# Packed words for PE and ScalarE: one word for 16 counting steps and one for four destination scores, unpacked in registers, in a four-layer graph network

## The chip, the cores and the metric

One NeuronCore of a Trainium2 chip runs the whole program. The metric is the device time of one execution in microseconds. The kernel is written instruction by instruction, with semaphores between the engines: PE (TensorE), DVE (VectorE), ACT (ScalarE), POOL (GpSimd) and SP (SyncE, which only issues DMAs).

## The reference, cut to what matters

There are 1875 nodes with 256 features and 60,000 edges (src, dst) sorted by dst. Each of four layers computes a graph operation and then x = layernorm(x + layer(x)). The change lies in the first layer and in the counting that serves the later ones:

```
feat = einsum('ni,rhid->rnhd', x, W)                 # 8 relations, 4 heads of 64
el = sum(feat[type, src] * attn_l[type], -1)         # score of the source
er = sum(feat[type, dst] * attn_r[type], -1)         # score of the destination
e = leaky_relu(el + er); alpha = softmax of e over the edges with the same dst
h = segment_sum(alpha * feat[type, src], dst)        # GAT layer
segment_sum(msg[src], dst)                           # layers 2 and 3: relation sums, mean
```

In layers 2 and 3 the kernel multiplies by a dense count matrix: for each destination, how many edges come from each source (two relations). This matrix is what the counting walk makes.

## The kernel before

**Windows and steps.** Destinations are taken in WINS = 118 windows of 16. The sorted edges are cut into STEPS = 586 steps of up to 128 edges; a step lies in one window, and the window of a step never falls and rises by at most one from step to step. The array WS (one number a step, the same on all partitions) holds the window of each step. The engines learn it by loading numbers from on-chip memory into their registers: `offsets(engine, step, n, most, table)` loads n numbers of a table with one instruction (line 361 of the profile).

**Order of the stages.** (1) Up to 53 us: loading and the tables of steps. (2) 53 to 154 us: the feature table (8 relations by 1875 rows) on PE, written to device memory. (3) 166 to 398 us: the destination scores. (4) 398 to 421 us: transposes and a few matmuls. (5) 421 to 994 us: the counting walk. (6) 994 to 1315 us: softmax and the weighted sums of the first layer. (7) To the end: the other layers with the count matrix, all dense.

**Destination scores.** PG = 4 columns of edges are a group, of which there are NG = 32. For each group PE broadcasts the keys of the edges into PSUM (`broadcast_keys(g)`, L1548 and L1550), DVE and ACT turn them into one-hots (L1038, L1042 on DVE; L602, L604 copy on ACT), and PE multiplies them with a piece of the table ERW of 12 columns (`er_group(g)`, L1562): SC = 5 matmuls for each of the four columns, or four from group 19 on; 19 x 20 + 13 x 16 = 588. Which piece is the window's: an offset of 12 columns times the window. The 20 offsets of a group are loaded as 32-bit numbers from the table OFFP, which DVE fills early (L935, L938). DVE sums the results (L1047).

**Counting walk.** For each step DVE makes two one-hots (L1068 with 128 columns, L1069 with 480) in a ring of AS = 8 and signals `a_oh`; PE multiplies them into the PSUM bank of the window (L1600). A ring of CBANKS = 4 banks serves the windows: before a step PE waits for `a_free` to be at least the window's number plus one, and takes bank (window + 1) mod 4. ACT reads the bank of a finished window (L630), clears the bank (L589) and signals `a_free`. ACT knows how many steps a window has from the table ENDS, of one number a window, eight to a load (L627). PE's table CT holds 512 times (window + 1) as 16-bit numbers, eight to a load. 8 steps stand ahead of a loop of 18 turns with AU = 32 steps each, and 2 behind it.

**Gathers.** Beside stages 3 to 5 POOL gathers rows of the feature table for the edges with indirect DMAs (L546, 469 in all) into a ring of NPL = 6 places. ACT copies the scores out of each place (`collect`, L585), which gives the place back to POOL and to SP, which writes the rows on (L417). ACT does its collects at fixed places of its own order: behind its copies of each group in stage 3, behind certain windows in the walk (`due`).

## Time and profile before

| what | value |
|---|---|
| timed runs, median | 2030.09 us (2027.18 to 2038.34, n = 3) |
| profiled execution, its own time | 2011.49 us |
| its span | 2009.8 us |
| mean granted clock of PE | 0.765 |
| busy: PE, DVE, ACT, POOL | 69%, 49%, 27%, 24% |
| chain that ended last: PE, DVE, issue | 54%, 18%, 17% |

Busy is what an engine's instructions took of the span; register instructions and loads into registers are not counted in it. "Issue" is time in which an engine waited for nothing that the profile shows. The chain is followed back from the last instruction to what released each. The rows ahead of the prediction are from the profiled execution.

### The profile page before, as it was taken

How to read it: one execution, taken by the hardware profiler on the slowest of the kernel's cores; microseconds unless marked ns; L12 is line 12 of the kernel's file. 1: busy time of each engine (PE TensorE's matmuls, PEld its weight loads, DVE VectorE, ACT ScalarE, POOL GpSimd, SP SyncE). 2: the span in 40 equal slices, each digit the busy share in tenths (PEclk: the TensorE clock that was granted, in tenths of full speed). 3: DMA queues.
4: the chain of work that ended last, by engine and by line, in shares of the span. 5: the costliest groups of instructions: out<-in, count | busy, mean ns of one | idle time of the engine just before them, and what ended most of it. 6: DMA issues, size and time to landing. Idle time of an engine off the chain costs nothing.

```text
span 2009.8 us, 21459 instructions
## 1 busy us (share of the span) xinstructions
PE 1387.4 (69%) x5399; PEld 735.2 (37%) x5400; DVE 978.3 (49%) x2436; ACT 552.5 (27%) x856; POOL 486.8 (24%) x517
## 2 busy tenths in 40 slices
PE   5894676576654444333418999978999989989930
PEld 3342343221111100000207777744444544554620
DVE  5413334246654444333398998864081460360636
ACT  1331222101222222222300000024775436427121
POOL 0005565531454566565300000000000000000022
PEclk9996555576665655555657999988999989989975
DMA  3534555531344555555406888600000010000022
GB/s 145 169 142 159 178 164 161 176 96 53 119 143 139 159 168 173 176 166 161 139 22 225 281 269 275 205 1 23 1 1 1 0 32 1 1 11 1 2 60 60
DMA packets 84507, 223.92 MB, mean 111 GB/s; under 512 B 18456, under 2 KB 27588, under 8 KB 83908
## 3 DMA queue, kind: packets, MB, share of 16 engines
q1 hardware_dynamic: 60452, 158.01, 22.7%
q0 software_dynamic: 23968, 64.77, 12.2%
q8 instruction: 53, 0.87, 0.2%
q14 instruction: 34, 0.28, 0.0%
HBM read 140.09 MB, written 82.63 MB: 111 GB/s over the span
## 4 chain that ended last, share of the span: by engine, by line
PE 54%; DVE 18%; issue 17%; another core or an unknown queue 5%; ACT 3%; DMA 2%; POOL 0%; SPq 0%; ACTq 0%; DVEq 0%; POOLq 0%
PE bank L1729 15%; PE bank L1666 11%; PE bank L1600 7%; PE bank L1519 5%; DVE arena L1069 5%; PE bank L1749 2%; DVE arena L1098 2%; PE bank L1548 2%; PE bank L1562 2%; PE bank L1713 2%; DVE arena L1068 1%; PE bank L1688 1%; PE bank L1818 1%; DMA arena<-in_xT 1%
## 5 line engine op out<-in xcount | busy, mean ns | idle before, releaser
L546 POOL DMA_INDIRECT arena<-feat_table,arena x469 | 450.1, 960 | 482.9 <-ACT arena L585 251.3
L1600 PE MATMUL bank<-arena 128*128 128x480 f16 x586 | 261.4, 550 | 309.9 <-issue 275.9
L1068 DVE TENSOR_SCALAR arena<-iota,arena 128x128 f16<-128x128 f16 x586 | 155.1, 265 | 302.8 <-PE bank L1600 205.6
L1729 PE MATMUL bank<-arena 128*128 128x472 f16 x1440 | 292.5, 367 | 9.3 <-DVE arena L1248 5.4
L1600 PEld LDWEIGHTS bank<-arena 128*128 128x128 f16 x586 | 60.3, 103 | 511.4 <-issue 510.9
L554 POOL DMA_INDIRECT arena<-al_table,edge_ends x15 | 14.4, 962 | 952.7 <-DMA al_table<-arena 948.4
L1666 PE MATMUL bank<-arena 128*128 x966 | 229.5, 392 | 0.7 <-issue 0.3
L1069 DVE TENSOR_SCALAR arena<-iota,arena 128x480 f16<-128x480 f16 x586 | 204.0, 348 | 0.0
L1729 PEld LDWEIGHTS bank<-arena 128*128 128x128 bf16 x1440 | 141.9, 99 | 159.7 <-issue 12.8
L1666 PEld LDWEIGHTS bank<-arena 128*128 128x128 f32 x966 | 174.5, 190 | 55.9 <-issue 34.6
L630 ACT ACTIVATE adjacency<-bank 128x480 uint16<-128x480 f32 x118 | 67.3, 570 | 442.3 <-PE bank L1600 382.6
L1154 DVE TENSOR_TENSOR arena<-arena 128x1024 f32<-128x1024 f32 x118 | 140.4, 1214 | 14.3 <-DMA arena<-edge_rows 12.6
L717 ACT ACTIVATE arena<-adjacency 128x1888 f16<-128x1888 uint16 x30 | 108.8, 3630 | 45.0 <-PE bank L1729 45.0
L698 ACT ACTIVATE arena<-adjacency 128x1888 f16<-128x1888 uint16 x30 | 109.0, 3637 | 34.6 <-PE bank L1729 34.6
L1519 PE MATMUL bank<-arena 128*128 128x512 f32 x240 | 111.3, 619 | 5.8 <-ACT arena L577 3.0
L1562 PE MATMUL bank<-arena 128*128 x588 | 76.8, 188 | 51.8 <-issue 46.2
L1548 PE MATMUL bank<-adjacency,ident 128*128 128x512 f16 x128 | 67.1, 617 | 42.1 <-DVE arena L1038 36.5
L1562 PEld LDWEIGHTS bank<-arena 128*128 128x128 f16 x588 | 59.3, 105 | 84.8 <-issue 72.7
L602 ACT ACTIVATE arena<-bank 128x512 f16<-128x512 f32 x64 | 35.7, 595 | 187.8 <-remote 122.2
L1161 DVE TENSOR_TENSOR arena<-iota,arena 128x1024 f32<-128x1024 f16 (+1 forms) x61 | 73.8, 1210 | 8.3 <-PE bank L1666 8.2
L1269 DVE COPY arena<-bank 128x472 f32<-128x472 f32 x12 | 7.0, 642 | 143.3 <-PE bank L1729 143.3
L1047 DVE TENSOR_REDUCE arena<-bank 128x80 f32<-128x240 f32 x32 | 13.0, 405 | 125.5 <-remote 85.8
(289 smaller groups left out, 1496.6 us busy)
## 6 DMA issues: line engine op xcount, KB each, us to landing
arena<-edge_rows SPq DMA_DIRECT2D x117, 520.0 KB, 4.7
edge_rows<-arena SPq DMA_DIRECT2D x67, 520.0 KB
edge_rows<-arena SPq DMA_DIRECT2D x67, 390.0 KB
feat_table<-arena SPq DMA_DIRECT2D x60, 260.0 KB, 2.1
arena<-feat_table,arena POOLq DMA_INDIRECT x469
arena<-in_w SPq DMA_DIRECT2D x1, 2048.0 KB, 9.7
arena<-in_xT SPq DMA_DIRECT2D x1, 1920.0 KB, 18.2
arena<-in_x SPq DMA_DIRECT2D x1, 1792.0 KB
```

What stands on the lines that cost most here:

```text
L546: g.indirect_dma_start(out=PLACE[k][:, t - lo, :], out_offset=None, in_=feat_t, in_offset=bass.IndirectOffsetOnAxis(ap=IE[:, t:t + 1], axi ...
L698: a.activation(chunk(CH1, c % 2, wide), ADJ[:, r, :].rearrange("p (n s) -> p n s", s=SH)[:, :, sh], ACT.Copy).then_inc(s["chunk_ready"], 1)
L717: a.activation(chunk(CH2, c % 2, wide), ADJ[:, 0, :].rearrange("p (n s) -> p n s", s=SH)[:, :, c], ACT.Copy).then_inc(s["chunk_ready"], 1)
L1068: v.tensor_scalar(OHS[st % AS], iota128[:, :], lo, None, ALU.is_equal)
L1069: v.tensor_scalar(OHK[st % AS], iota480[:, :], key, None, ALU.is_equal).then_inc(s["a_oh"], 1)
L1154: v.tensor_tensor(rows, rows, al, ALU.mult).then_inc(s["r_wgt"], 1)
L1519: ins = mm(PS[c][:, :], XT0[:, k, P * t:P * (t + 1)], W0[:, k, 512 * c:512 * (c + 1)], start=(k == 0), stop=(k == 1))
L1548: ins = mm(PS[j][:, 0:SFULL * P], row, KEY16[:, 0:SFULL, :].rearrange("p c e -> p (c e)"), start=True, stop=True)
L1562: ins = mm(PS[4 + g % 2][:, 3 * H * k:3 * H * (k + 1)], KO[g % 3][:, lo:lo + P], ERW[:, bass.ds(offs[k], 3 * H)], start=True, stop=True)
L1600: mm(CBANK[:, bass.ds(at, R2 * KW)], OHS[st % AS], OHK[st % AS], start=False, stop=False, skip_group_check=True)\
L1666: mm(BANKS[:, bass.ds(out_at, D)], OHR[:, (st // RG) % ORING, P * (st % RG):P * (st % RG + 1)], FBf[:, bass.ds(places[st % RK] >> 12, D)], ...
L1729: ins = mm(PS[4 * fo + j][:, 0:CW], m[:, P * fo:P * (fo + 1)], ch[:, CW * j:CW * (j + 1)], start=(c == 0 and q == 0), stop=(c == n - 1 and ...
```

## The change

**PE, counting.** CT becomes a 32-bit table with one word for CWORD = 16 steps, 38 words. Its low 7 bits are the window (plus one) of the first of these steps, and each of the 15 bits above says whether the window rises at the next step. PE adds the bits up in a register, step by step. A turn loads two words with one instruction. To make words and turns fit, the table begins 8 steps ahead of the first step. The bank's address is now worked out from the window: shift by 9, mask.

**PE, destination scores.** OFFP holds one word for the same matmul of the four columns of a group, four windows of 7 bits; five words a group are loaded, and PE shifts, masks and multiplies by 12.

**ACT.** ENDS holds two numbers of 12 bits in a word; a load takes four words for eight windows.

**DVE** makes the packed tables. OFFP and CT are now made ahead of the wait for `er_ld`, some 30 small operations; before, OFFP was made earlier (L935, L938) and CT after the scores (L1064).

```diff
-assert CBANKS >= 3 and AS % CLOAD == 0 and AU % CLOAD == 0 and 512 * WINS < 2 ** 16 and STEPS % 2 == 0 and CBANKS & (CBANKS - 1) == 0
+WBITS = 7
+WFULL = 2 ** WBITS
+CWORD = 16
+CROWS = -(-(STEPS + AS) // CWORD)
+EBITS = 12
...
-        CT = ar(A_WI, STEPS // 2).bitcast(U16)
+        CT = ar(A_WI, CROWS).bitcast(I32)
...
                 if w % CLOAD == 0:
-                    ends = nc.values_load_multi_w_load_instructions(
-                        ENDS[0:1, w:w + min(CLOAD, WINS - w)], engines=[ACTE], min_val=1, max_val=STEPS)[1]
-                act.wait_ge(s["a_mm"], ends[w % CLOAD])
+                    ends = offsets(ACTE, w // 2, min(CLOAD, WINS - w) // 2, STEPS * (2 ** EBITS + 1), ENDS)
+                act.wait_ge(s["a_mm"], ends[w % CLOAD // 2] >> (EBITS * (w % 2)) & (2 ** EBITS - 1))
...
-            v.tensor_copy(ENDS[0:1, 0:WINS], PS[4][0:1, 1:WINS + 1]).then_inc(s["ends_ready"], 1)
+            BEG = TMP[0:1, 1024:1024 + WINS]
+            link(v.tensor_copy(BEG, PS[4][0:1, 1:WINS + 1]))
+            BEGv = BEG.rearrange("p (w k) -> p w k", k=2)
+            v.scalar_tensor_tensor(ENDS, BEGv[:, :, 1], float(2 ** EBITS), BEGv[:, :, 0], ALU.mult, ALU.add).then_inc(s["ends_ready"], 1)
...
-            link(v.memset(OFFP, 0))
-            for c in range(SC):
-                n = min(P, STEPS - P * c)
-                v.tensor_scalar(OFFP.rearrange("p (a c) -> p a c", c=SC)[:, 0:n, c], WS[:, P * c:P * c + n], float(3 * H), None, ALU.mult)
...
+            OFFF = OFFW.rearrange("p c g j -> p (c g j)")
+            link(v.memset(OFFF, 0))
+            link(v.tensor_copy(OFFF[:, 0:STEPS], WS))
+            OPv = OFFP.rearrange("p (g c) -> p c g", c=SC)
+            OTv = OFFT.rearrange("p (g c) -> p c g", c=SC)
+            link(v.tensor_copy(OPv, OFFW[:, :, :, 0]))
+            for j in range(1, PG):
+                link(v.tensor_single_scalar(OTv, OFFW[:, :, :, j], WBITS * j, ALU.logical_shift_left))
+                link(v.tensor_tensor(OFFP, OFFP, OFFT, ALU.bitwise_or))
+            CWP = TMP[:, 640:640 + CWORD * CROWS]
+            CDF = TMP[:, 1280:1280 + CWORD * CROWS]
+            POW = TMP[:, 1920:1920 + CWORD]
+            link(v.memset(CWP, 0.0))
+            v.tensor_copy(CWP[:, CWORD - AS:CWORD - AS + STEPS], WS)
+            v.tensor_scalar(CWP[:, CWORD - AS + STEPS:CWORD * CROWS], CWP[:, CWORD - AS + STEPS:CWORD * CROWS], float(WINS - 1), None, ALU.add)
+            for u in range(CWORD):
+                ins = v.memset(POW[:, u:u + 1], float(WFULL * 2 ** (u - 1)) if u else 0.0)
+            link(ins)
+            v.memset(CDF[:, 0:1], 0.0)
+            link(v.tensor_tensor(CDF[:, 1:CWORD * CROWS], CWP[:, 1:CWORD * CROWS], CWP[:, 0:CWORD * CROWS - 1], ALU.subtract))
+            CDv = CDF.rearrange("p (b u) -> p b u", u=CWORD)
+            link(v.tensor_tensor(CDv, CDv, POW.rearrange("p (a u) -> p a u", a=1).to_broadcast([P, CROWS, CWORD]), ALU.mult))
+            link(v.tensor_reduce(CDF[:, 0:CROWS], CDv, AX.X, ALU.add))
+            v.scalar_tensor_tensor(CT, CWP.rearrange("p (b u) -> p b u", u=CWORD)[:, :, 0], 1.0, CDF[:, 0:CROWS], ALU.add, ALU.add)\
+             .then_inc(s["counts_table"], 1)
             dve.wait_ge(s["er_ld"], 16)
...
-            v.tensor_scalar(CT, WS, 1.0, 512.0, ALU.add, ALU.mult).then_inc(s["counts_table"], 1)
...
-                offs = offsets(PE, PG * SC * g, PG * SC, 3 * H * (WINS - 1), OFFP)
+                words = offsets(PE, SC * g, SC, WFULL ** PG - 1, OFFP)
...
+                        off = nc.s_assert_within((words[c] >> (WBITS * j) & (WFULL - 1)) * (3 * H), 0, 3 * H * (WINS - 1),
+                                                 skip_runtime_bounds_check_because="a window's number times the width of its scores")
                         ins = mm(PS[4 + g % 2][:, 3 * H * k:3 * H * (k + 1)], KO[g % 3][:, lo:lo + P],
-                                 ERW[:, bass.ds(offs[k], 3 * H)], start=True, stop=True)
+                                 ERW[:, bass.ds(off, 3 * H)], start=True, stop=True)
...
-            most = 512 * WINS
-
-            def count(i, st, word):
+            def count(i, st, window):
 
                 pe.wait_ge(s["a_oh"], i * AU + (st + 1))
-                pe.wait_ge(s["a_free"], word >> 9)
-                at = nc.s_assert_within(word & (512 * (CBANKS - 1)), 0, 512 * (CBANKS - 1), skip_runtime_bounds_check_because="a bank of the window's ring")
+                pe.wait_ge(s["a_free"], window)
+                at = nc.s_assert_within((window << 9) & (512 * (CBANKS - 1)), 0, 512 * (CBANKS - 1),
+                                        skip_runtime_bounds_check_because="a bank of the windows' ring")
                 mm(CBANK[:, bass.ds(at, R2 * KW)], OHS[st % AS], OHK[st % AS], start=False, stop=False, skip_group_check=True)\
                     .then_inc(s["a_mm"], 1)
 
-            words = offsets(PE, 0, AS, most, CT)
-            for st in range(AS):
-                count(0, st, words[st])
+            def count_word(i, word, st0, lo, hi):
+
+                window = word & (WFULL - 1)
+                for u in range(hi):
+                    if u:
+                        window = window + (word >> (WBITS + u - 1) & 1)
+                    if u >= lo:
+                        count(i, st0 + u, window)
+
+            most = 2 ** (WBITS + CWORD - 1) - 1
+            count_word(0, offsets(PE, 0, 1, most, CT)[0], -AS, AS, CWORD)
             with pe.Fori(0, A_N) as i:
-                for u in range(AU):
-                    if u % CLOAD == 0:
-                        words = offsets(PE, i * AU + (AS + u), CLOAD, most, CT)
-                    count(i, AS + u, words[u % CLOAD])
-            words = offsets(PE, AS + A_N * AU, STEPS - AS - A_N * AU, most, CT)
-            for st in range(AS + A_N * AU, STEPS):
-                count(0, st, words[st - AS - A_N * AU])
+                for k, word in enumerate(offsets(PE, i * 2 + 1, 2, most, CT)):
+                    count_word(i, word, AS + CWORD * k, 0, CWORD)
+            count_word(0, offsets(PE, 2 * A_N + 1, 1, most, CT)[0], AS + A_N * AU, 0, STEPS - AS - A_N * AU)
```

## Rows read from the trace of the kernel before

**Rows 1.** Busy time by stretch: us, then PE, PEld, DVE, ACT, POOL; PEclk, DMA, GB/s
```profile
166.00:398.00 232.00, 139.17 (x784) 79.86 (x782) 73.20 (x129) 48.00 (x121) 140.48 (x148) 0.51 0.55 171
421.00:575.00 154.00, 93.94 (x222) 22.77 (x220) 97.08 (x437) 22.63 (x56) 49.39 (x52) 0.64 0.28 88
575.00:994.00 419.00, 169.13 (x369) 38.13 (x369) 169.39 (x739) 108.13 (x264) 238.79 (x250) 0.56 0.51 160
```

**Rows 2.** Timeline of PE, early counting walk: start, duration, then the instructions
```profile
423.05 1.58 PE L1600 MATMUL bank<-arena 128*128 128x480 f16 x7
...
439.81 3.54 PE L1600 MATMUL bank<-arena 128*128 128x480 f16 x8 [1.96 <-issue]
445.26 3.54 PE L1600 MATMUL bank<-arena 128*128 128x480 f16 x8 [1.92 <-issue]
451.15 3.57 PE L1600 MATMUL bank<-arena 128*128 128x480 f16 x8 [2.35 <-issue]
```

**Rows 3.** PE's sequencer by source line: ns min/median/max of one, first and last start
```profile
L361 PEldq TENSOR_LOAD <-arena x74: 155/1922/2911, 419.5 to 992.8; - x74
...
L361 PEldq TENSOR_LOAD <-adjacency x32: 1356/1362/2438, 166.6 to 392.3; - x32
...
L361 PEldq TENSOR_LOAD <-arena x121: 330/333/779, 1071.8 to 1305.1; - x121
...
L1598 PEldq ALU_OP  x586: 2/36/1394, 421.8 to 993.7; - x196
...
L1600 PEldq ALU_OP  x586: 2/36/1395, 421.9 to 993.8; - x196
L1600 PEldq FUSED_REGOPS  x586: 1/46/1396, 422.0 to 993.9; - x196
...
L1562 PEldq FUSED_REGOPS  x588: 2/46/1397, 168.0 to 395.8; - x196
...
L1666 PEldq FUSED_REGOPS  x966: 42/60/103, 1073.1 to 1306.9; - x194
...
L1666 PEldq ALU_OP  x483: 32/32/32, 1073.3 to 1306.8; - x161
```

**Rows 4.** Groups: L1600 in 575 to 994, L630 over the span; busy, idle before
```profile
L1600 PE MATMUL bank<-arena 128*128 128x480 f16 x369 | 169.2, 559 | 250.1 <-issue 225.0 <-ACT bank L589 19.5 <-DVE arena L1069 4.6
...
L630 ACT ACTIVATE adjacency<-bank 128x480 uint16<-128x480 f32 x118 | 67.3, 570 | 442.3 <-PE bank L1600 382.6
```

**Rows 5.** Timelines of PE and of POOL in the late walk
```profile
765.65 0.56 PE L1600 MATMUL bank<-arena 128*128 128x480 f16 x1 [2.23 <-issue]
770.58 0.56 PE L1600 MATMUL bank<-arena 128*128 128x480 f16 x1 [4.37 <-issue]
...
751.00 0.94 POOL L546 DMA_INDIRECT arena<-feat_table,arena  x1 [1.68 <-issue]
...
771.41 0.94 POOL L546 DMA_INDIRECT arena<-feat_table,arena  x1 [0.30 <-issue]
```

**Rows 6.** Timeline of PE in the destination scores
```profile
207.00 2.76 PE L1562 MATMUL bank<-arena 128*128 x20 [0.91 <-DVE arena L1047]
...
211.79 2.31 PE L1562 MATMUL bank<-arena 128*128 x20
...
299.03 0.17 PE L1562 MATMUL bank<-arena 128*128 x1 [1.22 <-issue]
```

**Rows 7.** DVE before its first comparison, and the nearest prices (by source line)
```profile
164.28 1.42 DVE L1038 TENSOR_SCALAR arena<-bank,pcol 128x512 f16<-128x512 f32 x2 [0.83 <-PE bank L1550]
...
L935 DVE MEMSET adjacency<- x1: 592/592/592, 73.3 to 73.3; 128x640 int32 x1
...
L957 DVE TENSOR_TENSOR arena<-adjacency x1: 770/770/770, 87.4 to 87.4; 128x586 f32<-128x586 f32 x1
...
L1003 DVE TENSOR_TENSOR scores<-scores,iota x1: 261/261/261, 155.9 to 155.9; 1x110 int32<-1x110 int32 x1
```

**Rows 8.** DMA queues in the walk, 450 to 990: packets, MB, share
```profile
q14 instruction: 8, 0.07, 0.0%
```

More of the change, by code:

```diff
@@ L269, in build @@
         HB = ar(A_HB, D)
[L270 removed]
+        ENDS = ar(A_HB, WINS // 2)[0:1, :].bitcast(I32)
         OHR = ar(A_OR, ORING, RG * P)
@@ L274, in build @@
         KEY16 = EARLY[:, 47 * Q:47 * Q + SC * P // 2].bitcast(F16).rearrange("p (c e) -> p c e", e=P)
-        OFFP = EARLY[:, 45 * Q + 8:45 * Q + 8 + P * SC].bitcast(I32)
+        OFFW = TMP[:, 0:P * SC].bitcast(I32).rearrange("p (c g j) -> p c g j", c=SC, j=PG)
+        OFFP, OFFT = (EARLY[:, 45 * Q + 8 + NG * SC * k:45 * Q + 8 + NG * SC * (k + 1)].bitcast(I32) for k in range(2))
         ERF = EARLY[:, 48 * Q:48 * Q + WINS * H].rearrange("p (w h) -> p w h", h=H)
```

2 lines of the change are left out of this document (1 added, 1 removed).

## The prediction

> **What bounds the kernel now.** I read the windows by stage first. The change touches three stretches: the destination scores (166 to 398 us), the first part of the counting walk (421 to 575) and its rest (575 to 994) [rows 1]. In none of them is an engine full. PE is busy 139 of 232 us, 94 of 154 and 169 of 419, DVE less or about as much, and POOL, with its gathers, 140, 49 and 239. So the order of work inside a stretch decides, and the timeline shows it.
>
> In the early walk PE runs eight steps in 3.54 us and then stands 1.92 us before the next eight; where a turn of 32 ends, 2.35 us [rows 2]. Two things are to be seen. The eight steps are (3.54 - 0.58) / 7 = 0.42 us apart, although seven matmuls of the same form that had been queued up ran in 1.58 us, 0.2 us apart: the spacing in the loop comes from what PE's sequencer does between matmuls. And the pause of 1.92 us has the length of the median load of eight 16-bit words [rows 3]. A turn of 32 steps takes 3 x 5.45 + 5.89 = 22.2 us, 0.69 us a step; 154 us for 218 steps is 0.71. DVE's pair of one-hots and ScalarE's clearing follow PE there.
>
> The rest of the walk takes 419 / 368 = 1.14 us a step. PE idles 250 us before its matmuls, 225 of them "issue" [rows 4]: the engine waits for its own instruction stream. The timeline shows a second speed: at 765.65 and 770.58 single steps stand 4.9 us apart, within a run of 17 gathers on POOL, unbroken from 751.00 to 772.35, 20.41 / 16 = 1.28 us each [rows 5]. In the same way matmuls of the destination scores, usually 0.11 us apart, come at 1.4 us [rows 6]. Slow stretches occur only late in such long runs of gathers; early in the walk, with short runs, there are none. What is in them costs about 0.7 us for each instruction of PE's stream, whatever it does: 1.40 us for a matmul with one register instruction.
>
> **Price of a register instruction.** A destination-score matmul is preceded by one register instruction, a counting step by four (a sum for a_oh in line 1597, a shift in 1598, mask and address in 1600) [rows 3]. (2.31 - 0.19) / 19 = 0.11 us against 0.42, so each is (0.42 - 0.11) / 3 = 0.10 us. The 36 and 46 ns of the rows are the busy part only; three times 36 would give a step of 0.22 us, which is not seen.
>
> **Counting, early part.** After the change a step with u > 0 needs: the sum for a_oh, the shift, the mask with 1, the addition to the window, the shift by 9, the mask of the ring, the address: 7. The first step of a word needs 5. If the compiler folds pairs (in line 1666 one ALU and two fused instructions do the two addresses, shift and mask of two matmuls [rows 3]) it may be 5. I take 7, since the semaphore waits stand between the groups and a mask followed by an addition has no pair of that kind here. Turn after: 30 x 0.72 + 2 x 0.52 = 22.6, and in place of four loads at 1.92 one of two words; four 32-bit words take 0.33 [rows 3], and the branch 0.44 (2.35 - 1.92), so 23.4 us against 22.2. Over 218 steps, 6.8 turns, that is +8 us. Bounds: 5 instructions a step give 32 x 0.52 + 0.8 = 17.4 us, -32 us; 8 give +30.
>
> A page of the Trainium skill ("DMA: Bandwidth & Descriptors", the table of latencies and other measured facts) puts the floor of a tensor_load at about 600 ns. The trace has 0.33 us for four words, so it doesn't agree and the measurement decides. By the page each turn would be 0.27 us longer, an estimated +5 us over the 18 turns.
>
> **Counting, late part.** If x steps run at 4.2 us (six instructions by 0.7) and the others at 0.69, 4.2x + 0.69(368 - x) = 419 gives x = 47, or some 195 us of slow stretches. A slow step after has nine instructions, 6.3 us. If the slow time stays 195 us, 31 steps fall into it and 337 x 0.73 = 246 us follow: 441, +22. But POOL needs 250 x 1.28 = 320 us whatever PE does, PE in fast mode comes closer to its pace (0.73 us a step against 0.87 of gathers), and the runs of gathers, which start when ScalarE collects behind PE, may get shorter. I take +15, between 0 and +110 (all 47 steps stay slow: 47 x 2.1 = 99, and 11).
>
> **Destination scores.** A group of 20 matmuls takes 4.79 us now (207.00 to 211.79) [rows 6], one of 16 about 0.45 less; 19 and 13 of them are 147 us, and the stretch has 232: 85 us are slow. Added are a mask for the lowest number of a word, shift and mask for the three others: 1.75 x 0.10 = 0.175 us a matmul, 3.5 or 2.8 us a group (bounds 0, if all folds, and 3 instructions, 6 us). The load falls from 20 words, 1.36 us [rows 3], to five at about 0.35; half of it lies beside the broadcasts' matmuls, so -0.5. Fast groups then take 7.8 and 6.6 us, 234 us in all, as much as the stretch does now with its slow parts. POOL's part is 148 x 1.28 = 189 us; at 4.6 gathers, 5.9 us, a group it would no longer outrun PE, and its runs break up. With no slow time left the stretch stands still (+2). With half of it, 42 us at 2.6 us a matmul does only 16 of 588, +38. With all of it +75. I take +25, nearer to none, because the short runs of the early walk had none.
>
> **DVE's chain for the tables.** Some 30 small operations are put ahead of the wait for er_ld, and DVE waits only 0.83 us for PE before its first comparison at 164.28 [rows 7]. By their nearest rows: two memsets and two copies of some 600 numbers at no more than 0.59; a strided copy and six operations on 160 integers at 0.26; three passes over 608 at 0.77; the last 0.2: 6.7 us. For 16 memsets of one column the nearest row is the 0.26 of 110 integers, so 0 to 4 us; being one column each I take 0.05, 0.8. 7.5 less the 0.83: +6 (between 4 and 10). All that follows starts by so much later; PE's and ScalarE's first group wait for these comparisons. The operations taken out lay ahead of a wait of DVE for PE or beside PE's work: nothing.
>
> **ScalarE.** Its loads of eight words become loads of four, and each window has one or two register instructions more. It waits for PE 382 us in the walk [rows 4], so both are hidden while PE is the late one. In slow stretches its instructions too can cost 0.7, on one window in three of those steps; a few us, inside the bounds.
>
> **Sum.** 6 + 25 + 8 + 15 = +54 us. The profiled execution took 2011 us, the median of the timed runs is 2030, 0.9% more; 2011 + 54 = 2065 becomes 2084 against the median. I write 2085.
>
> **Rivals.**
> (a) The loads win: the compiler folds shift, mask and addition so that a step needs 5 and a matmul of the scores one or two. For it speaks line 1666. Early -32, late about -40 (368 / 218 of the early gain, less what the gathers hold), scores -5, DVE +6: -70, 1960; at 6 instructions a step about -20, 2010. It decides once a step has at most 6. Against it: word >> 9 and the ring's mask are two ALU instructions now, not folded.
> (b) The gathers set the pace: POOL's 1.28 us each bound both late stretches, and PE's added time falls into what were slow stretches. +6 +0 +8 -5, about +9: 2030 to 2040, no change to be told.
> (c) The slow stretches hold the same steps, each with more instructions at 0.7 us: +6 + 75 + 8 + 60 to 110, 2180 to 2230; half-way 2150. The price per instruction speaks for it; against it, that the runs of gathers end by POOL's own ring.
> (d) The turn's code grows from some 200 to some 290 instructions. In the walk there is practically no instruction traffic now, 8 packets [rows 8]: the turn stays resident. If it didn't, 18 turns would fetch; a pause like the longest load's, 2.9 us at most [rows 3], makes +50 us at the outside, on top of mine, 2135. "Runtime: NRT & Kernel Launch" of the Trainium skill, under Instruction fetch mechanics, says a taken branch to a page outside the window waits for a fetch; by the trace the rule has no case so far.
>
> **How the numbers follow.** My own case 0.54, with a range of 2043 (scores +2, late 0) to 2130; (a) 0.17; (b) 0.13; (c) 0.12; (d) 0.04. About 10 us, 0.5%, is what a measurement tells from no change. Faster 0.17, all of (a). Same 0.14: (b), and the edge of mine. Slower 0.69. The range of 8 in 10 leaves out the better half of (a) and the upper half of (c): 2005 to 2155.
>
> **What would show it.** Bursts of eight with pauses of 1.92 us are gone, and matmuls of line 1600's successor stand 0.72 us apart over 16 steps (0.5 would be rival a, and 0.42 free registers). The early walk takes about 162 us. Score matmuls stand 0.28 us apart in fast groups; the stretch from DVE's first comparison to the transposes is 235 to 270 us. DVE's first comparison starts near 170. Late single steps in long runs of gathers are 6 us apart; their total time tells (b), mine and (c) apart. Instruction-queue packets in the walk tell (d). I am wrong if a step has six register instructions or fewer, or if the slow stretches, which I know only by where they occur, answer to something else than the count of instructions.

## The result and the profile after

The changed kernel takes 2143.5 us (median; 2135.3 to 2151.2, n = 4) against 2029.8 us: ratio 1.056, 95% interval 1.051 to 1.060. It is 114 us slower. The forecast was +55 us (2085), so the side was right and the time stands within the range, but the loss is twice what was forecast. The profiled execution took 2135.3 us with a span of 2133.6, against 2011.5 and 2009.8: 124 us. That is 10 more than between the medians, because the profiled execution of the kernel before lies 18 us under its own median and that of the changed one 8 under; which stretch holds the 10 us can't be told.

From the page of the changed kernel: PE's clock in 40 slices, the chain that ended last by engine, and the gathers and the walk's matmuls (busy, mean ns, idle before and its releaser).

```profile
PEclk9995555565555555555555799999899989999975
...
PE 62%; issue 21%; DVE 13%; DMA 2%; ACT 1%; POOL 0%; SPq 0%; another core or an unknown queue 0%; DVEq 0%; ACTq 0%; POOLq 0%
...
L552 POOL DMA_INDIRECT arena<-feat_table,arena x469 | 449.1, 958 | 601.5 <-ACT arena L591 365.1
L1629 PE MATMUL bank<-arena 128*128 128x480 f16 x586 | 335.1, 576 | 289.6 <-issue 233.4
```

The same two groups of the kernel before:

```profile
L546 POOL DMA_INDIRECT arena<-feat_table,arena x469 | 450.1, 960 | 482.9 <-ACT arena L585 251.3
L1600 PE MATMUL bank<-arena 128*128 128x480 f16 x586 | 261.4, 550 | 309.9 <-issue 275.9
```

"Issue" has gone from 17 to 21% of the chain, PE from 54 to 62%. The matmuls of the walk are busy 335 us in place of 261, although they are the same matmuls. A little of it is the clock: more of them run at the lower one (mean 576 ns in place of 550, 586 x 26 ns = 15 us). The rest is how busy time is counted: at 0.42 us apart matmuls of 0.58 us overlap and the overlap counts once, at 0.73 us apart they don't overlap. POOL idles 119 us more, 114 of it until ScalarE's collects: the gathers are not what was late.

Windows that end with the first and the last matmul of each stretch tell where the 124 us are. First the changed kernel (scores, first 218 steps, the other 368; us, busy and count of these matmuls, granted clock, DMA share, GB/s), then the same stretches of the kernel before.

```profile
171.17:460.62 289.45, 102.64 (x588) 0.50 0.42 132
...
489.87:661.61 171.74, 123.25 (x218) 0.51 0.25 80
661.61:1114.64 453.03, 211.86 (x368) 0.50 0.47 146
```

```profile
168.12:396.08 227.96, 76.77 (x588) 0.50 0.54 169
...
423.04:579.01 155.97, 92.88 (x218) 0.63 0.28 90
579.01:994.64 415.63, 168.55 (x368) 0.56 0.51 159
```

Scores +61.5 us, first 218 steps +15.8, the others +37.4, together 114.7. The first score matmul starts 3.1 us later (168.12 to 171.17), between scores and walk there are 2.3 us more (29.25 against 26.96), and behind the walk 3.8 more. That makes 123.8.

DVE's first comparison, against [rows 7]:

```profile
167.16 1.41 DVE L1067 TENSOR_SCALAR arena<-bank,pcol 128x512 f16<-128x512 f32 x2 [0.83 <-PE bank L1578]
```

It starts 2.9 us later, with the same wait of 0.83 us.

The timeline of PE in fast groups of the scores (two groups of 16), and in the walk:

```profile
449.15 1.51 PE L1592 MATMUL bank<-arena 128*128 x6
450.83 1.17 PE L1592 MATMUL bank<-arena 128*128 x4 [0.17 <-issue]
...
455.58 1.59 PE L1592 MATMUL bank<-arena 128*128 x6 [1.43 <-DVE arena L1076]
...
499.73 1.29 PE L1629 MATMUL bank<-arena 128*128 128x480 f16 x2 [0.16 <-issue]
501.18 1.29 PE L1629 MATMUL bank<-arena 128*128 128x480 f16 x2 [0.17 <-issue]
```

Inside a word a score matmul now comes every (1.17 - 0.19) / 3 = 0.33 us (0.11 before), and a group of 16 every 6.4 us (449.15 to 455.58), a counting step every 1.45 / 2 = 0.73 us. The gaps say "issue".

The sequencer's rows, against [rows 3]: the scores' (L1592), then the sum for a_oh, the window's three instructions and its wait, and bank and address.

```profile
L1592 PEldq ALU_OP  x1029: 2/36/1388, 170.9 to 460.2; - x172
L1592 PEldq FUSED_REGOPS  x588: 2/55/709, 171.1 to 460.3; - x196
...
L1625 PEldq ALU_OP  x558: 1/36/1410, 493.2 to 1111.7; - x186
...
L1626 PEldq ALU_OP  x1692: 1/36/724, 483.3 to 1113.6; - x188
...
L1629 PEldq ALU_OP  x1172: 1/36/730, 485.1 to 1113.8; - x196
L1629 PEldq FUSED_REGOPS  x586: 1/46/723, 485.3 to 1113.9; - x196
```

1029 + 588 instructions for 588 matmuls are 2.75 each; 558 + 1692 + 1172 + 586 for 586 steps are 6.8 each. The compiler folded nothing of what I had left open.

The loads (two words at an odd place for the walk, four on ScalarE, five for the scores):

```profile
L367 PEldq TENSOR_LOAD <-arena x18: 3/534/909, 492.0 to 1070.7; - x18
L367 ACTq TENSOR_LOAD <-arena x14: 305/308/709, 584.8 to 1096.3; - x14
...
L367 PEldq TENSOR_LOAD <-adjacency x32: 584/1234/2045, 169.4 to 454.0; - x32
```

The two-word load takes 0.53 us and not 0.33, the five-word load 1.23 and not 0.35: it is hardly shorter than the 20 words before. Not every five-word load is that dear. The words of group g begin at word 5 x g of the table, and in e1 below, which has the same loads, those of g = 0, 4, 8 and so on to 28, which begin at a multiple of four words, take 0.59 to 0.63 us, and the 24 others 1.23 or more. This is the one of g = 4:

```profile
L367 PEldq TENSOR_LOAD <-adjacency x1: 601/601/601, 211.6 to 211.6; - x1
```

The late walk has slow stretches as before; this is the timeline of PE in one:

```profile
764.72 1.29 PE L1629 MATMUL bank<-arena 128*128 128x480 f16 x2 [0.17 <-issue]
768.95 0.58 PE L1629 MATMUL bank<-arena 128*128 128x480 f16 x1 [2.94 <-issue]
771.83 0.58 PE L1629 MATMUL bank<-arena 128*128 128x480 f16 x1 [2.31 <-issue]
775.95 0.56 PE L1629 MATMUL bank<-arena 128*128 128x480 f16 x1 [3.54 <-issue]
```

Single steps are 2.9 to 4.2 us apart, less than the 4.9 of [rows 5], though each now has seven register instructions in place of four. Over the last 368 steps, those that start more than 1.2 us after the one before, with no load between, number 51 in the trace before (155 us in all) and 73 in this one (222 us): 3.0 us each in both.

### The profile page after: what moved, and what is told of

Its sections match the earlier page's. It is cut to its first block, busy times and chain, and to the rows that moved or that the text cites. A ratio compares the mean times of both kernels' runs of the same rounds, so it can differ in the third digit from the quotient of the medians.

```text
span 2133.6 us, 24047 instructions
## 1 busy us (share of the span) xinstructions
PE 1489.2 (70%) x5399; PEld 743.5 (35%) x5400; DVE 1027.0 (48%) x2463; ACT 551.9 (26%) x856; POOL 485.9 (23%) x517
## 4 chain that ended last, share of the span: by engine, by line
PE 62%; issue 21%; DVE 13%; DMA 2%; ACT 1%; POOL 0%; SPq 0%; another core or an unknown queue 0%; DVEq 0%; ACTq 0%; POOLq 0%
PE bank L1762 14%; PE bank L1629 13%; PE bank L1699 10%; PE bank L1547 5%; PE bank L1592 4%; PE bank L1576 3%; DVE arena L1097 3%; PE bank L1782 2%; DVE arena L1126 2%; PE bank L1746 1%; PE bank L1721 1%; PE bank L1619 1%; PE bank L1851 1%; PE bank L1848 1%; DMA arena<-in_xT 1%
## 5 line engine op out<-in xcount | busy, mean ns | idle before, releaser
L1629 PE MATMUL bank<-arena 128*128 128x480 f16 x586 | 335.1, 576 | 289.6 <-issue 233.4
L1699 PE MATMUL bank<-arena 128*128 x966 | 228.6, 393 | 1.0 <-issue 0.4
L1097 DVE TENSOR_SCALAR arena<-iota,arena 128x480 f16<-128x480 f16 x586 | 208.9, 357 | 0.0
L1699 PEld LDWEIGHTS bank<-arena 128*128 128x128 f32 x966 | 175.4, 191 | 54.5 <-issue 32.7
L1592 PE MATMUL bank<-arena 128*128 x588 | 102.6, 188 | 130.7 <-issue 85.9
L1592 PEld LDWEIGHTS bank<-arena 128*128 128x128 f16 x588 | 59.8, 107 | 187.7 <-issue 181.8
L608 ACT ACTIVATE arena<-bank 128x512 f16<-128x512 f32 x64 | 34.9, 595 | 253.0 <-PE bank L1578 134.2
L1076 DVE TENSOR_REDUCE arena<-bank 128x80 f32<-128x240 f32 x32 | 13.0, 408 | 171.7 <-PE bank L1592 163.8
```

The lines of the kernel that those rows point to most:

```text
L1097: v.tensor_scalar(OHK[st % AS], iota480[:, :], key, None, ALU.is_equal).then_inc(s["a_oh"], 1)
L1592: ins = mm(PS[4 + g % 2][:, 3 * H * k:3 * H * (k + 1)], KO[g % 3][:, lo:lo + P], ERW[:, bass.ds(off, 3 * H)], start=True, stop=True)
L1629: mm(CBANK[:, bass.ds(at, R2 * KW)], OHS[st % AS], OHK[st % AS], start=False, stop=False, skip_group_check=True)\
L1699: mm(BANKS[:, bass.ds(out_at, D)], OHR[:, (st // RG) % ORING, P * (st % RG):P * (st % RG + 1)], FBf[:, bass.ds(places[st % RK] >> 12, D)], ...
```

## The experiments

Each run lists the lengths of three stretches, from the first to the last matmul, read as above. "Ratio" is to the kernel before on the same chip, with its 95% interval where there were several runs; each stretch is from one profiled execution. e5 to e8 compute layer 1 from other data and serve only to time the stages.

| kernel | us | ratio | scores | first 218 | other 368 |
|---|---|---|---|---|---|
| before | 2029.8 | 1 | 228.0 | 156.0 | 415.6 |
| changed | 2143.5 | 1.056 (1.051 to 1.060) | 289.5 | 171.7 | 453.0 |
| e1 only scores packed | 2073.3 | 1.026 (1.021 to 1.032) | 287.3 | 161.6 | 411.9 |
| e2 only walk packed | 2073.4 | 1.028 (1.023 to 1.033) | 227.6 | 169.5 | 455.5 |
| e3 32-bit words, 8 a load | 1992.3 | 0.988 (0.983 to 0.993) | 229.0 | 134.2 | 407.8 |
| e4 the same, 16 a load | 1995.8 | 0.988 (0.983 to 0.993) | 229.7 | 135.8 | 411.7 |
| e5 before, 134 gathers | 1772.6 | single run | 137.8 | 150.8 | 268.7 |
| e6 changed, 134 gathers | 1895.4 | single run | 241.5 | 159.9 | 275.6 |
| e7 before, thin gathers | 2034.5 | single run | 233.6 | 166.5 | 420.2 |
| e8 changed, thin gathers | 2147.1 | single run | 291.2 | 181.9 | 461.8 |
| e9 e3 + 3 register instructions | 2118.6 | 1.043 (1.040 to 1.046) | 233.6 | 184.6 | 482.5 |
| e10 e3, POOL 3 parts ahead | 1997.3 | 0.982 (0.978 to 0.986) | 217.6 | 132.6 | 429.3 |
| e11 e3, POOL 2 parts ahead | 1995.9 | 0.983 (0.978 to 0.988) | 215.0 | 135.1 | 413.5 |
| e12 changed, POOL 2 parts ahead | 2129.7 | 1.049 (1.046 to 1.052) | 271.9 | 171.1 | 457.4 |
| e13 e3, pause at each part | 2025.8 | single run | 226.8 | 119.4 | 431.0 |
| e14 changed, pause at each part | 2067.1 | single run | 232.9 | 171.4 | 415.9 |
| e15 e3, one wait for 2 steps | 1994.4 | 0.983 (0.979 to 0.986) | 232.7 | 129.4 | 408.4 |
| e16 e3, one wait for 4 steps | 1984.7 | 0.978 (0.973 to 0.983) | 232.3 | 129.5 | 403.0 |
| e17 e16, short pause | 1909.9 | 0.940 (0.937 to 0.943) | 215.4 | 113.0 | 351.1 |
| e18 e16, rare pause | 1920.6 | 0.946 (0.944 to 0.948) | 195.3 | 127.2 | 360.8 |

**e1 and e2: one part of the change at a time.**

e1 is the kernel before with the changed kernel's OFFP of words and the er_group() that unpacks them. e2 is the changed kernel with the OFFP of offsets, made where it was, er_group() and the ENDS of one number a word of the kernel before.

> Only the destination scores are packed; the counting walk and ScalarE's table are as before. Theory A (a register instruction costs 0.10 us between bursts, and the slow stretches under long runs of gathers keep most of their time): fast groups of 7.9 and 6.5 us, 235 us in all, and 50 to 85 us of slow time on top, as in the changed kernel; stage 285 to 300 us, total +60 to +70 over before. Theory B (the slow time of the scores' stage in the changed kernel came from what the other parts do): the stage is 235 to 250 us, total +5 to +20.

> Only the counting walk is packed. Theory A: +2 us for DVE's tables, +45 to +60 us in the walk, of it 5 to 12 in the first 218 steps. Theory B: the walk's loss follows from the scores' stage leaving gathers in another place of their order; then the walk alone costs +10 to +25.

Each part costs alone what it costs in the changed kernel: the scores 287.3 us (theory A), the walk 169.5 and 455.5 us (theory A). The ratios' parts, 2.6% and 2.8%, add up to nearly the 5.6% of both. Theory B, that one part drives the other, falls. The whole of e1 is 54 us above the 2019.1 of its own chip and not 60 to 70: the scores are 59 us longer, but they start 2 us earlier, 4 us less lie between scores and walk, and the walk is 2 us longer, which may be chance. The first 218 steps of e2 are 13.5 us longer, a little more than the 12 I had allowed.

**e3 and e4: what the loads alone cost.** The table in 32-bit words, one a step as before.

```diff
-        CT = ar(A_WI, STEPS // 2).bitcast(U16)
+        CT, CB = ar(A_WI, STEPS).bitcast(I32), WS.bitcast(I32)
...
-            v.tensor_scalar(CT, WS, 1.0, 512.0, ALU.add, ALU.mult).then_inc(s["counts_table"], 1)
+            link(v.tensor_scalar(CT, WS, 1.0, None, ALU.add))
+            link(v.tensor_single_scalar(CB, CT, CBANKS - 1, ALU.bitwise_and))
+            link(v.tensor_single_scalar(CB, CB, 9, ALU.logical_shift_left))
+            v.tensor_tensor(CT, CT, CB, ALU.bitwise_or).then_inc(s["counts_table"], 1)
...
-                pe.wait_ge(s["a_free"], word >> 9)
+                pe.wait_ge(s["a_free"], word & 127)
 e4 besides: the loop of a turn loads 16 words at a time (PLOAD = 16)
```

> Before, with the counting table in 32-bit words, one for each step and eight a load as before; window and bank are in separate bits, so a step has four register instructions as before. Theory A1 (the time of a load goes by bytes that are not whole words: 16-bit elements cost 0.24 us each, 32-bit words 0.064): a load of eight takes about 0.59 us in place of 1.92, a turn of 32 steps about 17 us in place of 22.2, the first 218 steps 115 to 120 us in place of 154; the whole 40 to 80 us faster. Theory A2 (a load takes about 1.9 us for eight registers whatever the type): no change, within 5 us. Theory C (the gathers set the pace of the late walk): the early part gains 35 us, the late part nothing, -25 to -35 in all.

> As the kernel with 32-bit words, but 16 words a load. Theory A1: a load of 16 about 1.10 us, 2 x 1.10 against 4 x 0.59 a turn; 0 to 3 us less over the whole walk. Theory A2: a load takes twice as long, no difference.

The sequencer's load and PE's timeline in e3:

```profile
L361 PEldq TENSOR_LOAD <-arena x30: 4/592/1078, 428.5 to 573.2; - x30
...
437.90 3.33 PE L1603 MATMUL bank<-arena 128*128 128x480 f16 x8 [0.79 <-DVE arena L1072]
442.02 3.51 PE L1603 MATMUL bank<-arena 128*128 128x480 f16 x8 [0.79 <-DVE arena L1072]
446.59 3.35 PE L1603 MATMUL bank<-arena 128*128 128x480 f16 x8 [1.06 <-DVE arena L1072]
```

A load of eight words is 0.59 us, as expected, and the pause between two bursts is 0.8 to 1.1 us, at whose end the trace names DVE's one-hot. The first 218 steps take 134 us (expected 115 to 120: DVE is now the one that ends the pause), the others 408: that is theory C, the early part gains 22 us, the late part 8. Theory A2 falls. The load of 16 words of e4:

```profile
L362 PEldq TENSOR_LOAD <-arena x36: 7/1107/1929, 430.2 to 939.9; - x36
```

It changes nothing. Both kernels are 1.2% faster than the one before, with 1 outside their intervals. So the loads could be had for a third of their price without a single register instruction more.

**e5 and e6: few gathers.** Only the first tile of each part is gathered; the edge rows of the others are left out.

```diff
-    return 16 * (hi - lo) * (m // NPL + 1)
+    return 16 * (m // NPL + 1)
...
-                for t in range(lo, hi):
+                for t in range(lo, lo + 1):
                     g.indirect_dma_start(...)
```

> Before, but POOL gathers only the first tile of each of the 134 parts, 134 gathers in place of 469, so that no long run of gathers is left; edge rows of the other tiles are left out, so layer 1 is computed from other data. Theory S (single instructions of PE's stream cost about 0.7 us only under long runs of gathers): destination scores 145 to 155 us in place of 228, the first 218 counting steps 150 us as now, the other 368 steps 250 to 262 us in place of 416. Rival S2 (the slow stretches come from something in PE's own program, such as its code or its loads): the stretches stay within 10% of now.

> The changed kernel with the same 134 gathers. Theory S: destination scores 230 to 240 us in place of 289, first 218 steps 160 to 167 us, the other 368 steps 270 to 280 us in place of 455. The difference to the kernel before with few gathers is then the pure price of the register instructions: about +85 us in the scores, +10 and +18 us in the walk. S2: within 10% of now.

Windows of e5, then of e6 (scores, first 218 steps, the others):

```profile
169.12:306.87 137.75, 74.58 (x588) 0.51 0.49 174
...
329.19:480.01 150.82, 91.74 (x218) 0.64 0.16 57
480.01:748.72 268.71, 160.07 (x369) 0.60 0.44 157
```

```profile
175.38:416.92 241.54, 107.99 (x588) 0.50 0.26 95
...
439.98:599.87 159.89, 121.69 (x218) 0.52 0.14 53
599.87:875.44 275.57, 212.11 (x368) 0.50 0.44 154
```

Theory S holds and S2 falls. Before: 137.8 and 268.7 us in place of 228.0 and 415.6, so 90 and 147 us come with the gathers. Changed: 241.5 and 275.6 in place of 289.5 and 453.0, so 48 and 177. I call these differences slow time. They hold the slow steps and whatever else the missing gathers would have cost. The slow steps themselves are gone: matmuls of one score group that are more than 0.5 us apart number 45 before and 51 in the changed kernel, and 1 in either kernel with few gathers. The pure price of the register instructions, with the shorter loads in it, is +103.8 us in the scores (expected 85), +9.1 in the first 218 steps (expected 10) and +6.9 in the others (expected 18).

**e7 and e8: thin gathers.** Each gather fetches rows of 4 numbers from another place of the table, so layer 1 is computed from other data.

```diff
-                    g.indirect_dma_start(out=PLACE[k][:, t - lo, :], out_offset=None, in_=feat_t,
+                    g.indirect_dma_start(out=PLACE[k][:, t - lo, D:FW], out_offset=None, in_=feat_t.rearrange("n (a b) -> (n a) b", b=H),
```

> Before, with all 469 gathers, but each fetches rows of 4 numbers in place of 260 (from another place of the feature table, so layer 1 is computed from other data). SP's writes are as they were. Theory I (the slow stretches come with the issue of a gather, 128 descriptors each, whatever it moves): scores and walk within 5% of now, slow steps with 4 to 5 us between them remain. Theory D (they come from the data that the gathers move): scores 145 to 170 us, last 368 steps 260 to 330 us.

> The changed kernel with thin gathers. Theory I: scores about 289 us and last 368 steps about 455 us, within 5%. Theory D: scores 235 to 250 us, last 368 steps 275 to 350 us.

Theory I: with a 65th of the gathers' bytes scores and late walk are within 3% of the full gathers. PE's timeline in e7 still has its slow steps (this one comes 5.6 us after the step at 720.70):

```profile
726.33 0.56 PE L1600 MATMUL bank<-arena 128*128 128x480 f16 x1 [5.06 <-issue]
```

So it isn't the data that the gathers move. SP's writes of the rows were left as they were; no run takes them out alone. (The first 218 steps even took 10 us more in both, for which I have no reason.)

**e9: register instructions alone.**

```diff
-                pe.wait_ge(s["a_free"], word & 127)
+                pe.wait_ge(s["a_free"], (((word & 127) << 9 >> 9) & 255) & 127)
```

> The kernel with 32-bit words and eight of them a load, plus three register instructions a step that change nothing (a pair of shifts, two masks of the window), so 7 in place of 4 as in the packed walk; no packed tables. Theory P (it is the number of register instructions that costs, 0.10 us outside and about 0.7 us inside the slow stretches): step 0.72 us apart, the first 218 steps about 175 us (132.7 before the additions, 169 in the packed walk), the other 368 steps 440 to 460 us against 409; +65 to +85 us over the kernel without the three. Rival Q (the packed walk lost its time late through the chain of the window from step to step or through its loads, and the number of instructions is hidden by the gathers there): the other 368 steps stay at 405 to 420, +40 us in all.

The first 218 steps take 184.6 us and the others 482.5: +50.4 and +74.7 us against e3. Theory P is right in its side and was too small in its size: 482.5 us where 440 to 460 were expected, and 184.6 where about 175. Q falls. Over the 218 steps an added instruction costs 50.4 / 654 = 0.077 us, over the 368 steps 74.7 / 1104 = 0.068: somewhat less than the 0.10 between matmuls, early and late alike, probably since part of it lies in pauses.

With this the change to the walk comes apart into three steps, first 218 and other 368: shorter loads of the same number (before to e3) -21.8 and -7.8; three register instructions more (e3 to e9) +50.4 and +74.7; 20 loads in place of 74 (e9 to e2) -15.1 and -27.0. The last step also holds 0.2 of a register instruction a step less (6.8 in place of 7), an estimated 3 and 5 us at the prices just found. The loads together give -36.9 and -34.8, the registers +125.

**e10 to e12: POOL less far ahead.**

```diff
+                if m >= RUN:
+                    pool.wait_ge(s["collected"], m - RUN + 1)
 RUN = 3 in e10, 2 in e11 and e12
```

> The kernel with 32-bit words; POOL may be only three parts of 3 or 4 gathers ahead of ScalarE's collects in place of six, so an unbroken run has at most 11 gathers, 14 us, in place of 21, 27 us. Theory R (a slow stretch begins some 6 to 12 us into an unbroken run of gathers, so shorter runs have less of it): scores 190 to 215 us in place of 228, last 368 steps 340 to 390 in place of 409, 40 to 90 us faster than with six parts. Rival R2 (slow time goes by the number of gathers, however they are spaced, or the shorter ring starves POOL): no gain, or up to 60 us slower.

> The same with two parts ahead, at most 7 gathers, 9 us, to a run. Theory R: hardly any slow stretch left; scores 150 to 200 us, last 368 steps 300 to 370, unless POOL now waits for ScalarE each time: 469 gathers of 1.28 us are 600 us, and a hand-over of 2 to 3 us at every second part makes 130 to 200 us more, so the last steps may be held by the gathers, near 400. Rival R2: 30 us or more slower than with six parts.

> The changed kernel with two parts ahead, to see what of its loss lies in slow stretches. Theory R: scores 240 to 255 us in place of 289, last 368 steps 300 to 400 in place of 455; the whole 60 to 110 us faster than the changed kernel. Rival R2: within 2% of the changed kernel, or slower.

By the numbers R falls and R2's "no gain" holds: nothing clear beyond e3 (0.982, 0.983 against 0.988), with 11 to 18 us less in the scores and 4 to 21 more in the late walk; the loss of 30 us that R2 gave e11 didn't come. But the runs hadn't become short. POOL and then PE in e11:

```profile
759.63 0.94 POOL L549 DMA_INDIRECT arena<-feat_table,arena  x1 [8.00 <-ACT arena L588]
...
776.11 0.94 POOL L549 DMA_INDIRECT arena<-feat_table,arena  x1 [0.30 <-issue]
```

```profile
768.37 0.58 PE L1606 MATMUL bank<-arena 128*128 128x480 f16 x1 [2.45 <-issue]
...
775.47 0.56 PE L1606 MATMUL bank<-arena 128*128 128x480 f16 x1 [3.67 <-issue]
```

Here are 14 gathers without a break (759.63 to 777.05), because ScalarE collects while POOL goes on, and PE slows down from about 765 to about 779. So these runs don't tell R from R2.

**e13 and e14: a pause ahead of each part.** All 469 gathers, in runs of 3 or 4.

```diff
+                for r in range(8):
+                    g.memset(ST[:, :, :], 0.0).then_inc(s["rest"], 1)
+                    pool.wait_ge(s["rest"], 8 * m + r + 1)
                 for t in range(lo, hi):
                     g.indirect_dma_start(...)
```

> The kernel with 32-bit words; ahead of each part of 3 or 4 gathers POOL does eight small chained memsets, an estimated 2 us in all (204 ns each is the nearest memset of the trace before), so no run of gathers is longer than 4, 5 us; all 469 gathers remain. Theory R (slow stretches need an unbroken run of more than some 6 us): no slow stretches; destination scores 140 to 190 us, held by the gathers if at all; the walk is then held by POOL, 469 x 1.28 + 134 x 2 = 870 us from the first gather, so the whole may well be slower. Rival N (slow time goes by the number of gathers, 0.6 us of it to each): single steps 3 to 5 us apart remain, scattered.

> The changed kernel with the same pauses. Theory R: destination scores 240 to 250 us, and first to last step of the walk no longer than in e13 within 30 us, since both wait for POOL. Rival N: scores about 289 us, and the walk 60 us or more longer than that of e13.

POOL in e13, and the scores of e14 (windows):

```profile
802.32 1.06 POOL L550 DMA_INDIRECT arena<-feat_table,arena  x1 [0.30 <-issue]
803.38 1.81 POOL L547 MEMSET ln_stats<- 128x90 f32 x8
805.46 0.95 POOL L550 DMA_INDIRECT arena<-feat_table,arena  x1 [0.27 <-ACT arena L589]
```

```profile
170.65:403.53 232.88, 104.72 (x588) 0.50 0.47 149
```

The scores of e14 take 232.9 us in place of 289.5, no longer than with few gathers (241.5). Score matmuls of a group more than 0.5 us apart number 4 in place of 51. Theory R stands: N would have left 289 us. The changed kernel gets from 2143 to 2067 us by a break of 2.1 us on POOL at each part.

In e13 the expectation for the scores failed: 226.8 us, not 140 to 190, though the slow matmuls are gone there too (1 in place of 42), and the whole is slower than e3 (2025.8 against 1992.3). The waits of e13, in the scores and then in the last 368 steps, tell why (us, times, longest):

```profile
ACT arena L589 <- DMA arena<-feat_table,arena: 168.6, 34, 8.0
...
ACT arena L589 <- DMA arena<-feat_table,arena: 281.5, 64, 6.5
PE bank L1607 <- ACT bank L593: 238.0, 59, 7.5
```

ScalarE now waits for the gathered rows before each collect, with its copies and the clearing of banks behind it, and PE waits for those. The breaks made the gathers the bound. In the scores of e14, where PE has more to do, ScalarE waits only 5.7 us for gathers. The late walk takes 415.9 us in e14 and 431.0 in e13: the one with nearly twice the register instructions is not slower, since both wait for POOL (ScalarE 226 and 282 us for gathers). Of the 41 us between e14 and e13 the first 218 steps have +52 and the scores +6, against -15 in the late walk and -10 between scores and walk; the walk as a whole is 37 us longer, a little more than the 30 I had allowed.

**e15 and e16: fewer register instructions.**

```diff
-                pe.wait_ge(s["a_oh"], i * AU + (st + 1))
+                if st % 4 == 0:
+                    pe.wait_ge(s["a_oh"], i * AU + min(st + 4, STEPS))
 e15 the same with 2
```

> The kernel with 32-bit words; PE waits for DVE's one-hots once for two steps, so every second step has one register instruction less: 3.5 a step in place of 4. Theory P: 0.05 us x 586 = 29 us less between bursts where DVE's 0.41 us pair doesn't hold it, and late 0.7 x 0.5 in each slow step; together -10 to -30 us against the kernel without. Rival D (DVE's pair and the hand-over are the bound once the loads are short): 0, or up to 10 us slower, for PE waits for two pairs.

> The same once for four steps, 3.25 instructions a step. Theory P: -15 to -40 us. Rival D: half the ring of eight one-hots has to be full before PE starts, so 10 to 40 us slower than with one wait a step.

Against e3 the walk is 4.3 us shorter with 2 and 9.6 with 4, in one profiled execution each. The ratios are 0.983 and 0.978 against 0.988 on another chip; the interval of e15 overlaps that of e3, that of e16 ends at 0.9827 where e3's begins at 0.9834. I count e15 as inconclusive and e16 as a gain of some 1% at most, with D at least half right: once the loads are short DVE ends most pauses. The timeline of e16 shows a second limit:

```profile
440.20 2.70 PE L1604 MATMUL bank<-arena 128*128 128x480 f16 x8 [0.83 <-DVE arena L1072]
...
757.49 3.38 PE L1604 MATMUL bank<-arena 128*128 128x480 f16 x8 [0.53 <-DVE arena L1072]
```

At 440 the granted clock is 1.00 (2.4 GHz), at 757 it is 0.50 (1.2 GHz). With 3.25 register instructions the steps are (2.70 - 0.36) / 7 = 0.33 us apart at the full clock and (3.38 - 0.58) / 7 = 0.40 at half of it. With four, in e3, they are 0.42 apart at either (3.33 us for eight steps at a clock of 1.00, 3.51 at 0.50 to 0.62). So the register instructions set the 0.42, and an instruction less gives nearly nothing where the clock is low, as it is in most of the late walk (0.57 over it in e3).

**e17 and e18: a shorter and a rarer pause.** On e16.

```diff
 e17
+                for r in range(3):
+                    g.memset(ST[:, :, :], 0.0).then_inc(s["rest"], 1)
+                    pool.wait_ge(s["rest"], 3 * m + r + 1)
 e18
+                for r in range(8 if m % 2 == 0 else 0):
```

> 32-bit words, one wait for four steps, and POOL does three chained memsets ahead of each part, about 0.95 us with the gap behind them (8 took 1.81 us + 0.27). Theory R: no run is longer than 5 us, so no slow stretches, if a gap of 1 us is long enough; the gathers then take 469 x 1.25 + 134 x 0.95 = 714 us against 854 with the long pause: destination scores 160 to 200 us, the walk 440 to 490 us, the whole 1880 to 1950 us. Rival G (the gap must be as long as the 2 us and more in which a slow stretch ends after a run): slow stretches as in e16, the whole 1970 to 2010 us.

> The same with eight memsets, 2.1 us, ahead of every second part, so runs of 7 gathers, 9 us; gathers 469 x 1.25 + 67 x 2.1 = 727 us. Theory R: part of the slow stretches comes back, since they begin 6 to 12 us into a run; the whole 1900 to 1970 us. Rival G: about 1900, for here the gap is long enough and the run nearly short enough, and e17 is the slower one.

Both beat every other kernel here: 1909.9 us, 6.0% less than before, and 1920.6, 5.4% less. The late walk takes 351 and 361 us in place of 403, the scores 215 and 195 in place of 232. Slow steps remain in e17, as here in its scores:

```profile
208.44 0.21 PE L1569 MATMUL bank<-arena 128*128 x2 [1.23 <-issue]
209.18 0.17 PE L1569 MATMUL bank<-arena 128*128 x1 [0.54 <-issue]
```

Score matmuls of a group more than 0.5 us apart number 33 in e16, 28 in e17 and 5 in e18. In the last 368 steps PE's register instructions longer than 0.25 us number 192, 59 and 33. So a gap of 1 us does less than one of 2.1 us, even though e18 has runs of 7 gathers and e17 of 4: G is right about the slow steps, most of all in the scores, where e17 is above what I expected (160 to 200). It is wrong in the sum, for e17 isn't the slower one: the longer gap is also paid in the pace of the gathers. In the late walk PE waits 100 us in e17 and 123 in e18 until ScalarE clears a bank, 10 in e16.

## Why the prediction was right in side and wrong in size

**The price of a register instruction held.** 0.10 us each gave 0.72 us a step and, over the 1.75 instructions that a score matmul has more on the average, 0.28 us a matmul. The trace has 0.73 us a step. With few gathers score matmuls come 0.124 us apart before (e5), and in the changed kernel (e6) 0.226 with the mask alone and 0.327 with shift and mask: 0.10 us for each. Nothing was folded: 6.8 instructions a step and 2.75 a matmul, against my 7 and 2.75. Rival (a), that the loads win, falls by its own condition.

**DVE's chain**, +6: the first comparison moved by 2.9 us, but the other traces show that this profile is a favourable one. The first score matmul starts at 170.7 to 175.4 us in the five kernels that have the whole chain and at 166.0 to 169.2 in the thirteen that have none of it, 172.7 and 167.7 on the average. The term is +5 and held. Here part of it was offset by a feature table that was done 5 us earlier.

**First 218 steps**, +8: +15.8. With few gathers it is +9.1, the term as I had worked it out. The rest is slow time, 5 us before (156.0 against 150.8) and 12 after.

**Destination scores**, +25: +61.5. This is the step that failed, twice. The pure price was +104 and not +87: I let the load of five words cost 0.35 us by the four-word row, and three in four of them cost 1.23. And I wrote that POOL "would no longer outrun PE, and its runs break up", so that little of the slow time was left. e5 and e6 show 48 us of it left, of 90. A pause on POOL takes it out (e14: 289.5 to 232.9), so it was this.

**The other 368 steps**, +15: +37.4. Here too the step failed. By my terms the registers would cost 368 x 0.30 = 110 us and the 46 loads that go with these steps would give 84 back, 4 x 1.92 us a turn less one short load. The runs show +75 for the registers and only -35 for the loads. Making the loads 1.33 us shorter (e3) gave 8 us of the 61 that 46 of them add up to; in its place slow steps without a load grew from 51 (155 us) to 82 (210 us), so what the loads give back the gathers take. That the gathers are behind this is shown by their absence: with few of them the change costs these steps +6.9 us, with all of them +37.4, so the slow time grew from 147 to 177 us. For an unchanged slow time I had worked with 31 slow steps in place of 47, each half as long again; the trace has 73 in place of 51, each as long as before.

**The price in a slow stretch** was wrong. "A slow step after has nine instructions, 6.3 us" is not what the trace has: 3.0 us on the average, as before. The time of a slow step doesn't go by the number of its instructions.

**Rivals.** (b), the gathers set the pace, is wrong for this change, for POOL waited 114 us longer for the collects; in e13, with its breaks, the gathers do set the pace. (c) gives a number close to the result, 2150, but for a reason that falls with the price in a slow stretch; right in it is only that the slow stretches remain, 48 us of them in the scores and 177 in the late walk. (d), code that no longer stays resident, falls; in the walk there are as many instruction packets as in [rows 8]:

```profile
q14 instruction: 8, 0.07, 0.0%
```

The rule of the Trainium skill that a taken branch outside the window waits for a fetch ("Runtime: NRT & Kernel Launch", Instruction fetch mechanics) again had no case: the traces show 8 packets of this queue in the walk of either kernel. The floor of about 600 ns that the Trainium skill gives for a tensor_load ("DMA: Bandwidth & Descriptors", Latency and other measured facts) doesn't agree with 0.31 us for four words on ScalarE and 0.53 for two on PE; the measurement decides.

**What stays open.** Why PE's sequencer slows down in a long run of gathers. It needs the run unbroken (e13, e14), it doesn't need the bytes (e7, e8), and it isn't PE's program (e5). PE isn't alone in it: in the last 368 steps before, 10 of ScalarE's 94 register instructions took more than 0.25 us too, and none with few gathers, while none of DVE's 390 did in either. (In the changed kernel none of ScalarE's 146 did.) What the gathers of POOL share with the register instructions of the others isn't shown by any run here. Why the slow steps became more and not longer is open as well.

## What to carry to other kernels

Count the register instructions of an engine as work: here each took 0.10 us of PE's time between matmuls of 0.2 to 0.6 us, and three more of them for each step (+125 us) outweighed the saving of nearly all loads (-72 us). Before packing a table look at what makes its load dear: 32-bit words in place of 16-bit ones cut the same load to 0.59 us with no other cost. And where an engine's "issue" time sits under long runs of gathers, try a break in the runs; a break of 1 us at each part was worth more (from 1985 to 1910 us) than anything done to the engine itself. Its length has to be tried: with 2.1 us at each part the gathers became the bound, and a kernel of 1992 us took 2026.

## What the runs showed of the hardware that was not expected

- A load into registers goes by width and place, not by count alone. Loads of whole groups of four 32-bit words take 0.33 us for 4 words, 0.59 for 8, 1.11 for 16 and 1.36 for 20, about 0.065 us a word. Five words take 0.59 us where they begin at a multiple of four words and 1.23 elsewhere. The 1.23, the 0.53 of two words that begin at an odd place and the 1.92 of eight 16-bit numbers all fit 0.31 us for the first number (a load of one word takes that) and 0.23 for each further one.
- Late in unbroken runs of gathers, of 1.25 us each, PE's stream nearly stands: counting steps are 3.0 us apart on the average (up to 4.9 in the rows shown) in place of 0.4 or 0.7, with four or seven register instructions alike. Breaks of 2.1 us after 3 or 4 gathers remove nearly all of it, breaks of 1 us only a part; in e11 a run of 14 was enough to have it from its sixth gather on.
- POOL's memset of 128x90 numbers, chained to the next by a semaphore, takes 1.81 / 8 = 0.23 us, which makes it a pause of fine grain.
